# One batch's sends in a row, slots a step earlier, early pad rows, and half tiles in a four-layer kernel

## What is computed

```python
x = x + tanh(g_xattn[0]) * L0_xattn(layernorm(x), ctx)      # one head, 32 keys
x = x + tanh(g_ffn[0])   * L0_ffn(layernorm(x))             # 8 heads, each attends among its own 64 chosen tokens
x = x + tanh(g_xattn[1]) * L1_xattn(layernorm(x), ctx, mask)# 16 heads, 32 keys
x = x + tanh(g_ffn[1])   * L1_ffn(layernorm(x))             # 8 experts, top 2 of each token, and a shared expert
```

## Time and profile before

| | |
|---|---|
| median of three runs | 331.97 us |
| the profiled execution's own time | 333.4 us |
| its span | 331.6 us |
| busy: PE, PEld, DVE, ACT, POOL | 246.3, 188.1, 221.9, 195.1, 168.4 us |
| mean granted TensorE clock | 0.892 |
| selected-token stage | about 78 to 115 us |
| third layer and routing | about 115 to 206 us |
| last send issued, first expert rows landed | 220.4, 227.5 us |
| last expert rows written | 314.2 us |

### The profile page before, as it was taken

One profiled execution on the slowest core, in us unless ns is written; L12 is line 12 of the kernel. 1 busy time (PEld: TensorE's weight loads), 2 busy tenths in 40 slices (PEclk: granted clock), 3 DMA queues, 4 the chain that ended last, 5 costly groups with the idle time before them and its releaser, 6 DMA issues.

```text
span 331.6 us, 6994 instructions
## 1 busy us (share of the span) xinstructions
PE 246.3 (74%) x2113; PEld 188.1 (57%) x2113; DVE 221.9 (67%) x687; ACT 195.1 (59%) x454; POOL 168.4 (51%) x208
## 2 busy tenths in 40 slices
PE   2887770797999788998987925414999999998600
PEld 2773240355777465677756712212799999997400
DVE  2487078995677666688899766700577767676555
ACT  2753599687677688976864444200676666764220
POOL 2513199931222564741106777750068888787521
PEclk9999996799999999999999555755999999999965
DMA  7880003420000000000000111433123222211093
GB/s 202 239 354 6 1 1 123 141 102 0 3 1 2 0 3 1 2 0 2 1 2 33 42 41 54 124 100 81 35 74 91 76 61 82 78 37 32 1 285 95
DMA packets 21458, 21.64 MB, mean 65 GB/s; under 512 B 3360, under 2 KB 19106, under 8 KB 20784
## 3 DMA queue, kind: packets, MB, share of 16 engines
q1 hardware_dynamic: 18784, 16.79, 16.8%
q0 software_dynamic: 2496, 4.26, 4.0%
q10 hardware_dynamic: 144, 0.15, 0.2%
HBM read 14.68 MB, written 7.42 MB: 67 GB/s over the span
## 4 chain that ended last, share of the span: by engine, by line
PE 31%; POOL 19%; DVE 19%; issue 15%; ACT 7%; DMA 5%; SPq 0%; POOLq 0%; DVEq 0%; ACTq 0%
PE bank L1148 25%; POOL expert_rows L818 12%; POOL dispatched_rows L794 6%; DVE region_p L897 2%; DVE x L1139 2%; DVE region_k L884 2%; DMA region_q<-expert_rows 2%; DVE top L883 2%; DVE nm L970 1%; DVE region_k L972 1%; DMA dispatched_rows<-region_t,slot 1%; PE bank L1355 1%; POOL rstd L736 1%; DVE bn_raw L843 1%; DMA x<-in 1%
## 5 line engine op out<-in xcount | busy, mean ns | idle before, releaser
L1148 PE MATMUL bank<-w_scaled,w_high 128*128 128x256 f16 x276 | 48.2, 279 | 1.0 <-ACT w_scaled L689 1.0
L818 POOL DMA_INDIRECT expert_rows<-region_k,slot_dest x24 | 29.5, 1229 | 28.1 <-DVE region_k L1121 21.1
L794 POOL DMA_INDIRECT dispatched_rows<-region_t,slot x32 | 32.6, 1019 | 16.6 <-issue 9.2
L1148 PE MATMUL bank<-w_high,region_k 128*128 (+1 forms) x308 | 32.3, 224 | 8.5 <-DVE region_k L1088 7.0
L1148 PE MATMUL bank<-w_scaled,w_low 128*128 128x256 f16 x138 | 38.4, 278 | 0.0
L689 ACT ACTIVATE w_scaled<-bank 128x512 f16<-128x512 f16 x23 | 13.7, 597 | 38.0 <-PE bank L1450 37.9
L1124 DVE TENSOR_TENSOR region_k<-region_x,region_k 128x768 f16<-128x768 f32 x23 | 22.0, 958 | 19.0 <-ACT region_k L694 19.0
L1148 PEld LDWEIGHTS bank<-w_high,region_k 128*128 128x128 f16 x308 | 25.7, 100 | 10.9 <-DVE region_k L1088 8.4
L818 POOL DMA_INDIRECT expert_rows<-region_x,slot_dest x22 | 27.3, 1241 | 6.7 <-issue 6.7
L745 POOL TENSOR_TENSOR w_low<-w_scaled,w_high 128x512 f16<-128x512 f32 (+1 forms) x23 | 27.8, 1236 | 5.5 <-ACT w_high L523 5.3
L1148 PEld LDWEIGHTS bank<-w_scaled,w_high 128*128 x276 | 26.5, 100 | 4.5 <-issue 1.3
(11 more groups left out here) (236 smaller groups left out, 708.5 us busy)
## 6 DMA issues: line engine op xcount, KB each, us to landing
w_scaled<-in SPq DMA_DIRECT2D x5, 1024.0 KB, 8.2
w_scaled<-dispatched_rows SPq DMA_DIRECT2D x23, 131.0 KB, 2.3
region_q<-expert_rows SPq DMA_DIRECT2D x4, 512.0 KB, 5.6
dispatched_rows<-pad_rows SPq DMA_DIRECT2D x18, 65.5 KB, 2.7
x<-in SPq DMA_DIRECT2D x4, 256.0 KB, 4.5
region_w<-in SPq DMA_DIRECT2D x2, 512.0 KB, 7.3
out<-x SPq DMA_DIRECT2D x4, 256.0 KB, 2.5
w_scaled<-in SPq DMA_DIRECT2D x1, 704.0 KB, 4.1
```

The lines of the kernel that those rows point to most:

```text
L794: pool.indirect_dma_start(disp, bass.IndirectOffsetOnAxis(slot[:, b * T + t, c:c + 1].bitcast(U32), 0), pay[:, b * T + t, :], None).then_i ...
L818: pool.indirect_dma_start(ytok, bass.IndirectOffsetOnAxis(dst[:, n, h:h + 1].bitcast(U32), 0), yv[n % 4][:, h * D:(h + 1) * D], None, boun ...
L1148: return pe.matmul(o, l, r, start=start, stop=stop)
```

## The change

1. `C_POOL`: the first batch's second half of sends moves from 19.1 to 15.6, right behind its first half; the other batches keep theirs.
2. `C_DVE`: `slots` moves from 12 to 11. The four instructions for the gates leave the last `slots` and follow the tile table.
3. SP writes pad rows over all of the dispatch table, all 9 regions, in nine DMAs, ahead of the sends; the 16 small ones behind the counts go, and `pad_row_i` with them. POOL's first send waits for the pads. SP loads the first two row numbers before it waits for the sends.
4. Selected-token stage: scores as two products 64x64, one for each batch's diagonal block; mixing products with 64 rows, batch i into bank 6 + i. Both banks now hold columns of two groups, and the first mix of group g waits for the low half of group g - 1.
5. At the end batch 2 is loaded, added and stored in four token tiles, behind batches 0, 1 and 3.

```diff
-         "shift_logits": 10.4, "route": 10.9, "slots": 12}
-C_POOL = {"rstd": -4.6, "early_low": -5.3, "low": -0.9, "rstd2": 6.5, "send": 12.5, "send2": 16.1}
+         "shift_logits": 10.4, "route": 10.9, "slots": 11}
+C_POOL = {"rstd": -4.6, "early_low": -5.3, "low": -0.9, "rstd2": 6.5, "send": 12.5, "first_send2": 12.6, "send2": 16.1}
...
+        def mixed(g):
+
+            c = g % 2 * 2 * D
+            return psum[:, 6 * 512:8 * 512].rearrange("p (i n) -> p i n", i=2)[:, :, c:c + 2 * D].rearrange("p i (h d) -> p i h d", h=2)
...
-            for h in range(2):
-                eng.dma_start(disp[E * REG + h * P:E * REG + (h + 1) * P, :], padt[:, :]).then_inc(padded, 16)
+            for e in range(E + 1):
+                n = (REG if e < E else TP) // P
+                eng.dma_start(disp[e * REG:e * REG + n * P, :].rearrange("(n p) w -> p n w", p=P),
+                              padt[:, :].rearrange("p (n w) -> p n w", n=1).to_broadcast((P, n, PAY_W))).then_inc(padded, 16)
 
             eng.wait_ge(tiles, 1)
-            for e in range(E):
-                row = eng.value_load(padr[0:1, e:e + 1], min_val=0, max_val=E * REG)
-                for h in range(2):
-                    eng.dma_start(disp[ds(row + h * P, P), :], padt[:, :]).then_inc(padded, 16)
-            eng.wait_ge(padded, 16 * (2 * E + 3))
+            rows = [eng.value_load(trow_i[0:1, n:n + 1], min_val=0, max_val=E * REG) for n in range(AHEAD)]
+            eng.wait_ge(w_low_done, CHUNKS)
             eng.wait_ge(sent, 16 * 2 * NT)
-            eng.wait_ge(tiles, 2)
-
-            eng.wait_ge(w_low_done, CHUNKS)
...
-            for b in range(B):
+            for b in (*range(B - 2), B - 1):
...
-            eng.wait_ge(stored, 16 * B)
+            for t in range(T):
+                n = (B - 2) * T + t
+                eng.wait_ge(sum_done, B - 2 + t + 1)
+                eng.dma_start(out_v[:, n:n + 1, :], x[:, n:n + 1, :]).then_inc(stored, 16)
+            eng.wait_ge(stored, 16 * (B - 1 + T))
...
                 elif stage == "send" and t % T == T - 1:
+                    pool.wait_ge(padded, 16 * (E + 2))
...
-                elif stage == "send2" and t % T == T - 1:
+                elif stage == ("send2" if b else "first_send2") and t % T == T - 1:
...
+            for u in range(T):
+                t = (B - 2) * T + u
+                dve.wait_ge(rows_loaded[u], 16 * len(range(u, TILES, 4)) + 16)
+                link(dve.scalar_tensor_tensor(x[:, t, :], yk[:, t, 0:D], gate[:, t, 0:1], x[:, t, :], ALU.mult, ALU.add))
+                dve.scalar_tensor_tensor(x[:, t, :], yk[:, t, D:2 * D], gate[:, t, 1:2], x[:, t, :], ALU.mult,
+                                         ALU.add).then_inc(sum_done, 1)
...
-                    mm(o, qkt[:, q, 0:P], qkt[:, q, P:2 * P], False, True).then_inc(slot_scores, 1)
+                    for i in range(2):
+                        r = slice(i * J, (i + 1) * J)
+                        last = mm(o[r, r], qkt[:, q, r], qkt[:, q, P + i * J:P + (i + 1) * J], False, True)
+                    last.then_inc(slot_scores, 1)
...
-                        wait(pe, mixed_low, g - 1)
+                        wait(pe, mixed_low, g)
                     for i in range(2):
-                        b = 2 * h + i
-                        last = mm(bank[6 + g % 2][J * (e % 2):J * (e % 2 + 1), b * D:(b + 1) * D],
-                                  etl[:, q, i * J:(i + 1) * J], vv[:, q, :])
+                        r, c = slice(i * J, (i + 1) * J), (2 * (g % 2) + h) * D
+                        last = mm(bank[6 + i][J * (e % 2):J * (e % 2 + 1), c:c + D], etl[r, q, r], vv[r, q, :])
```

More of the change, by code:

```diff
@@ L37 @@
 TTAB = 4 * ROUNDS + 8
+AHEAD = 2
 PAY_W = D + 3
@@ L254, in build @@
         te_i = sb("tile_pack_i", [P, ROUNDS], I32)
-        padr = sb("pad_row_i", [P, E], I32)
         onee = sb("ones_e", [P, E])
@@ L482, in _ @@
                 wait(eng, dest_ready, n - 3)
-                row = eng.value_load(trow_i[0:1, n:n + 1], min_val=0, max_val=E * REG)
+                row = rows[n] if n < AHEAD else eng.value_load(trow_i[0:1, n:n + 1], min_val=0, max_val=E * REG)
                 eng.dma_start(xd[:, n % 4, :, :], disp[ds(row, TP), :].rearrange("(h p) w -> p h w", p=P)).then_inc(rows_loaded[n % 4], 16)
@@ L486, in _ @@
                 eng.wait_ge(rows_sent[r], 32 * len(range(r, TILES, 4)))
-            for b in (0, B - 1, *range(1, B - 1)):
+            for b in (0, B - 1, *range(1, B - 2)):
                 eng.dma_start(yk[:, b * T:(b + 1) * T, :], ytok_v[:, b * T:(b + 1) * T, :]).then_inc(x_loaded[b], 16)
-            for b in range(B):
+            for t in range(T):
+                n = (B - 2) * T + t
+                eng.dma_start(yk[:, n:n + 1, :], ytok_v[:, n:n + 1, :]).then_inc(rows_loaded[t], 16)
+            for b in (*range(B - 2), B - 1):
                 if b < B - 1:
@@ L620, in _ @@
                     act.wait_ge(slot_mixed, n + 1)
-                    act.activation(yh[:, g, :, :].rearrange("p b d -> p (b d)"), bank[6 + g % 2][:, :], ACT.Copy).then_inc(mixed_high, 1)
+                    act.activation(yh[:, g, :, :].rearrange("p (h i) d -> p i h d", i=2), mixed(g), ACT.Copy).then_inc(mixed_high, 1)
             for stage, t in skewed(NT, C_EVERY, C_ACT):
@@ L943, in _ @@
                     dve.wait_ge(mixed_high, g + 1)
-                    dve.tensor_tensor(yl[:, g, :, :].rearrange("p b d -> p (b d)"), bank[6 + g % 2][:, :],
-                                      yh[:, g, :, :].rearrange("p b d -> p (b d)"), ALU.subtract).then_inc(mixed_low, 1)
+                    dve.tensor_tensor(yl[:, g, :, :].rearrange("p (h i) d -> p i h d", i=2), mixed(g),
+                                      yh[:, g, :, :].rearrange("p (h i) d -> p i h d", i=2), ALU.subtract).then_inc(mixed_low, 1)
             dve.wait_ge(layer1_loaded, 128)
@@ L1048, in _ @@
             link(dve.tensor_copy(cnt[:, :], bank[6][:, 0:E]))
-            dve.tensor_tensor(padr[:, :], cnt[:, :], c32[:, C_EREG:C_EREG + E], ALU.add).then_inc(tiles, 1)
             link(dve.tensor_scalar(cnti[:, :], cnt[:, :], float(TP - 1), None, ALU.add))
@@ L1133, in _ @@
             shared_dve(SH, B)
-            for b in range(B - 1):
+            for b in range(B - 2):
                 dve.wait_ge(x_loaded[b], 32)
@@ L1481, in down @@
                 last.then_inc(down_made, 1)
-            pe.wait_ge(tiles, 3)
+            pe.wait_ge(tiles, 2)
             load_window(0)
```

9 lines of the change are left out of this document (4 added, 5 removed).

## The result

The changed kernel takes 336.7 us (median of 4 runs, 335.36 to 338.92) beside 332.43 us of the kernel before on the same chip (4 runs): ratio 1.0132, 95% interval 1.0088 to 1.0175. It is slower by a little over 1%, where 332.9 us was forecast; the time lies in the range (328.2 to 337.0), and this side had a chance of 0.18. Its profiled execution took 337.84 us, span 336.0; TensorE's mean granted clock is 0.824, before it was 0.892.

The account below looks back on a forecast made before the run. No single engine was taken to bound the kernel (PE 31%, POOL 19%, DVE 19% of the chain). Terms +2.4 + 1.3 + 0 - 1.75 - 0.5 - 0.5 gave +0.95 us, median 332.9 us, range 328.2 to 337.0.

Parts of the forecast that it names:

- The waits: Selected-token stage: PE stands still 1.45 us for DVE's low half at three first mixes; +4.3 us, low end 2.
- Half tiles: Selected-token stage: half scores and half mix gain 0.12 us in each of 16 steps, -1.9 us; scores counted as 0.
- rival A: Selected-token stage: mode changes add a 0.17 us gap per step, halves don't overlap; +2.7 for -1.9, 337.5 us; chance 0.15.
- Rival B: Selected-token stage: the halves overlap in full and steps fall by 0.3 us to 1.73; 330.0 us; chance 0.2.
- The stage as a whole: Selected-token stage: waits of +4.3 and half tiles of -1.9 together make it 2.4 us longer.
- rival C: TensorE's clock falls only after the last statistics, work up to 192.96 gains 3.7 us; 329.2 us; chance 0.2.
- the clock level after 182 us: TensorE's granted clock after 182 us, where it was 1.2 GHz before: listed as a sign the prediction was wrong.
- Slots: Third attention, DVE: slots made one step earlier, right behind the routing, cost +1.3 us (0 to +2.5).
- First batch's sends: POOL: four sends go ahead of a norm in idle time, twenty stay behind the last norm; 0 us.
- Pads and row number: Last send to first expert rows: landing without pad transfers -1.75 us, row number loaded ahead -0.5 us.
- Four tiles: End of kernel: third batch's sums +0.4 us, smaller last store -0.9 us; -0.5 us in all.
- Sum: Whole kernel: all terms together +0.95 us, a median of 332.9 us.

Follow-up runs that it names:

- e2: Kernel before with only the wait changed: a group's first mix waits for DVE's low half of the group just before, full tiles, old banks; ratio 1.0149.
- e7: Kernel before with only the slots one step earlier (12 to 11), the gates staying with them; ratio 1.0027.
- e3: Kernel before with the change's selected-token stage (half scores, half mix), but each group's first mix issued one step later; ratio 1.0072.
- e4: Kernel before with only pad rows written early in nine transfers, row numbers loaded ahead and the third batch summed in four tiles; ratio 0.987.
- e11: Changed kernel with half scores kept but the old mix (128 rows, banks in turn, old wait); ratio to the kernel before 0.9935.
- e9: Kernel before with the edits of e4 and e8 together; slots, sends, gates and full mix as before; ratio 0.9866.
- e5: Changed kernel without its selected-token part (full tiles and the old wait); ratio to the kernel before 0.9959.
- e8: Kernel before with only the scores as two half tiles, 64x64 in place of 128x128, full mix; ratio 0.9919.
- e1: Kernel before with only the change's selected-token stage: half scores, half mix in both banks, wait for the low half; ratio 1.0194.

## Where the prediction was right and where wrong, point by point

- **The waits**, +4.3: right. PE is idle for DVE three times, 4.6 us in all, and the three steps are 1.6 us longer than the others, 4.8.
- **Half tiles**, 16 x 0.12 = -1.9: right in sign, the size low. The step fell by 0.22 to 1.82, over 13 steps -2.9. The gain is the mix's: from its start to the next turn of exp it went from 0.58 to 0.37, below the bound of 0.40. The 0 for the scores held, but for another reason than I gave. They got shorter (0.44 to 0.34), and the gaps around them took it back: 0.09 us more ahead of them, and 0.09 more behind them than where a mix of 128 rows follows. Together that is about the 0.17 of rival A, yet the step got shorter, since the mix gained more than that. With the rule of the Trainium skill that the prediction cites, TensorEngine Tiling (Array Packing), section Tiling Modes, that a change of tiling mode drains the engine, the trace agrees: both late starts stand where the tile changes its size. Rival B's step of 1.73 us didn't come.
- **The stage as a whole**, +2.4: the term that failed, though the time lies in the range. By waits and tiles it is +1.9, and the row says +5.8. I added up the time in which PE stands still and took the speed of all other products as given. The clock cost the rest: +1.1 in the step at 102 us and +2.6 behind the stage. That it comes with the waits is shown by e2; in the kernels with the half mix their share and that of the half tiles aren't parted. I looked at the clock only where it might bring a gain (rival C), not where the change makes idle time. My sign of being wrong, "the clock level after 182 us", was set too late in the kernel.
- **Slots**, +1.3: right, +0.9 in e7 and +1.1 in the changed kernel; the far side, 0.7 taken back in e7's run of sends, I had not counted. In the changed kernel the clock fell ahead of norm 2 too (norm 1-2 +1.6; e3, with slots at 12, shows the same 17.46 with the same fall). Falls near 170 us also stand in traces where this stretch isn't longer, so it isn't tied to an edit.
- **First batch's sends**, 0: right for what they buy, twenty still stand behind norm 3. I wrote that the eight end when the norm is due; that holds only with the earlier slots, and costs 2.9 us without them.
- **Pads and row number**, -2.25: -2.4 in both traces, with the pad writes done within 120 to 128 us, as forecast, and free of cost in the stage. That is in part luck. I took the old landing, 4.15 us, from one execution; in the six other kernels that keep the old pads and slots it took 2.69 to 3.33, and the last send to the first rows 5.72 to 6.42 us and not 7.15. Against those the early pads and row number (4.59 to 4.91) are worth 0.8 to 1.8 us. The run of sends was 0.35 shorter besides.
- **Four tiles**, -0.5: right, -0.6 (e4) to -0.8; the waits between sums cost 0.36.
- **Sum**: without the clock, 4.8 - 2.9 + 1.1 - 0.35 - 2.4 - 0.8 = -0.5 us by the traces, against +0.95 forecast, so the other terms were if anything too dark. The clock put 1.1 + 2.6 on it in and behind the stage, and 1.6 + 1.7 in places that the runs don't tie to the change; 2.1 of that came back in the stretch ahead of the change. The time lies near rival A's 337.5, but not for A's reason: no step without a wait was longer than 2.03 us at the full clock.

The experiments agree with this: the stage's part 1.0194 times the rest 0.9959 is 1.0152, and the changed kernel has 1.0132. e11 against the changed kernel says that the half mix with its wait costs 2.0%. The fastest versions are e4 (0.987) and e9 (0.9866); e5, e8 and e11 are below the kernel before too.

Two bounds belong to all this. The median of e1's six executions (334.95 to 341.75) is 4 us above its own profiled one, the fastest of them, so its other executions lost more than the trace shows; where, isn't known. Without its two longest (341.58 and 341.75) the median is 337.8, 1.3% above the kernel before, so 1.0194 is a rough price. Nor was it tried to keep the two groups in a bank apart by columns alone, without the wait: ACT's read and PE's write would be in one bank. The Trainium skill, PSUM — Partial Sum Buffer, section PSUM bank collisions raise a hardware error, says that two engines on the same bank and rows at once collide even at other columns; no run here shows it, and it is why a wait on the group just before stands there.

## What to carry to other kernels

A wait put into a stage in which TensorE is busy throughout costs its length, and here the clock of what follows fell as well: look for both, and read the granted clock behind the stage before and after. A product that gets cheaper is worth what the next product's start gains, gaps around it included: here half scores and half mix saved 0.16 and 0.21 us of a step alone and 0.22 together. And what an edit gains in its stage can be lost behind it: the half mix with its delay gained 1.7 us there, gave back 2.0 by the clock, and measured 1.0007, while the half scores kept TensorE busy and measured 0.9919. Work moved ahead of a norm on an in-order engine is free only until that norm is due: move what feeds it first.

## What the hardware did that I had not expected

- Pad writes at a DMA share of 1.25 to 1.31 for some 50 us beside the stage left its steps at 30.03 us (e4).
- Four passes of 64 rows and 64 columns (mix) take 0.44 us where those of 128 rows took 0.65. Two half scores behind a mask product of 128 columns start 0.09 us later than a full one.
- The time to the stage, in kernels that are alike up to there, runs from 78.55 to 81.12 us. The changed kernel was among the early ones although its clock was at the lower level where that of the kernel before was at the higher:

```profile
16.00:24.00 8.00, 6.95 (x41) 5.59 (x37) 6.75 (x31) 4.90 (x14) 1.59 (x4) 0.50 0.93 374
```

It read 1.00 there before, with PE busy 6.95 of 8.00 too. The two don't belong together: e5 had 0.50 there and came to the stage at 80.56, e1 had 1.00 and came at 79.00. The spread says that a single trace can't price anything under 2 us by its span. A stretch can be better, if it is seen to repeat (to norm 1: 46.63 to 46.66 us in all fourteen); the one from the last send to the first rows, 5.72 to 7.47 us in the eight kernels with the old pads, doesn't.
